# A graph network's sort with half of its keys in PSUM, its lists transposed ahead of the last raw products, and 14 raw rows instead of 11

## The reference

```python
h = relu(layernorm(x))
h = batchnorm(h, g0, b0)
for W1, b1, g, bt, W2, b2 in layers:        # two layers
    agg = segment_sum(h[src], dst, n)       # over the edges
    h = h + agg
    h = relu(batchnorm(h @ W1 + b1, g, bt))
    h = relu(h @ W2 + b2)
return x + h
```

## Time and profile before

| what | value |
|---|---|
| median of the runs | 2820.61 us |
| the profiled execution's own time | 2806.54 us |
| its span (first to last instruction) | 2804.7 us |
| busy: PE, DVE, ACT, POOL | 85%, 62%, 19%, 66% of the span |
| DMA | 735.46 MB, mean 262 GB/s |

### The profile page before, as it was taken

How to read it: one execution, slowest core, us unless ns; L and a number is a source line. 1 busy time by engine, 2 the same in 40 slices (tenths; PEclk the granted TensorE clock), 3 DMA queues, 4 the chain that set the end, 5 groups by cost and what they waited for, 6 DMA issues and landing times.

```text
span 2804.7 us, 30481 instructions
## 1 busy us (share of the span) xinstructions
PE 2380.3 (85%) x10221; PEld 1829.1 (65%) x10221; DVE 1734.9 (62%) x3349; ACT 528.8 (19%) x1542; POOL 1846.7 (66%) x1870
## 2 busy tenths in 40 slices
PE   1466657999999999999998666799999999989879
PEld 1133424788777777777776544588888888776767
DVE  6999995655555555555556577655555555544459
ACT  8963534300000000000007611100000000000038
POOL 2058886777777777777770277777777777777720
PEclk8685766999999999999998899999999999999999
DMA  9387994888888888888874999988888888888868
GB/s 307 144 263 203 300 311 123 254 267 254 254 254 254 254 254 253 254 254 254 253 242 161 338 354 353 301 282 288 284 284 287 284 283 287 259 254 254 253 204 271
DMA packets 309073, 735.46 MB, mean 262 GB/s; under 512 B 41126, under 2 KB 183346, under 8 KB 308910
## 3 DMA queue, kind: packets, MB, share of 16 engines
q0 software_dynamic: 148896, 552.17, 62.7%
q1 hardware_dynamic: 160014, 181.25, 20.0%
HBM read 580.67 MB, written 152.59 MB: 261 GB/s over the span
## 4 chain that ended last, share of the span: by engine, by line
PE 49%; DMA 21%; POOL 13%; SPq 7%; issue 5%; ACT 5%; DVE 1%; DVEq 0%; ACTq 0%; POOLq 0%
PE agg_ps L815 33%; DMA rows<-node_rows,src_all 19%; POOL rows L687 8%; SPq L610 7%; PE mm_ps L940 6%; PE mm_ps L857 5%; POOL rows L672 3%; PE mm_ps L861 2%; POOL raw_more L672 2%; ACT acc L985 2%; ACT lane_code L972 1%; PE agg_ps L769 1%; ACT lane_code L961 1%; DMA raw_more<-node_rows,src_all 1%; DMA node_rows<-acc 1%
## 5 line engine op out<-in xcount | busy, mean ns | idle before, releaser
L687 POOL DMA_INDIRECT rows<-node_rows,src_all x1672 | 1580.4, 945 | 647.6 <-issue 347.9
L815 PE MATMUL agg_ps<-rows,work 128*128 128x256 f32 (+1 forms) x7106 | 1662.4, 387 | 179.7 <-DMA rows<-node_rows,src_all 136.0
L815 PEld LDWEIGHTS agg_ps<-rows,work 128*128 128x128 f32 x7106 | 1311.0, 190 | 502.9 <-DMA rows<-node_rows,src_all 122.9
L1514 DVE SCALAR_TENSOR_TENSOR acc<-agg_ps,in_first,acc 128x256 f32 (+1 forms) x289 | 140.0, 485 | 955.9 <-PE agg_ps L815 880.7
L1016 ACT ACTIVATE bn_root<-bn_var 128x2 f32<-128x2 f32 x3 | 0.6, 204 | 1891.1 <-DVE bn_var L1146 1891.1
L672 POOL DMA_INDIRECT rows<-node_rows,src_all x96 | 137.2, 1429 | 166.2 <-DMA node_rows<-acc 137.2
L1466 DVE TENSOR_TENSOR work<-lane_code,lane_ps 128x1024 f32<-128x1024 f32 (+1 forms) x209 | 231.6, 1108 | 1.1 <-issue 1.1
L940 PE MATMUL mm_ps<-early,work 128*128 128x256 f32 x784 | 176.1, 389 | 20.0 <-ACT work L1095 11.4
L940 PEld LDWEIGHTS mm_ps<-early,work 128*128 128x128 f32 x784 | 141.0, 194 | 55.3 <-issue 23.4
L1475 DVE TENSOR_TENSOR work<-lane_code,lane_ps 128x640 f32<-128x640 f32 x209 | 169.8, 812 | 0.0
L1095 ACT ACTIVATE work<-acc,bn_shift,bn_scale 128x128 f32<-128x128 f32 x392 | 167.3, 485 | 3.3 <-DVE bn_shift L1157 2.8
(11 more groups left out here) (250 smaller groups left out, 1663.7 us busy)
## 6 DMA issues: line engine op xcount, KB each, us to landing
node_rows<-acc SPq DMA_DIRECT2D x113, 260.0 KB, 5.7
rows<-node_rows,src_all POOLq DMA_INDIRECT x1768, 4.3
node_rows<-acc SPq DMA_DIRECT2D x27, 910.0 KB, 4.3
node_rows<-acc SPq DMA_DIRECT2D x57, 390.0 KB, 5.9
node_rows<-acc SPq DMA_DIRECT2D x28, 650.0 KB, 7.7
node_rows<-acc SPq DMA_DIRECT2D x114, 130.0 KB, 4.6
acc<-in_x SPq DMA_DIRECT2D x13, 896.0 KB, 11.0
rows<-in_x SPq DMA_DIRECT2D x13, 896.0 KB, 7.4
```

Source lines behind the costliest of these rows:

```text
L687: pool.indirect_dma_start(tile_rows(k, 0, ROWS_OF[t] * DP), None, tables[layer][0:NPOS if t >= LAST_STRIDED else TABLE, :], bass.IndirectO ...
L815: mm = pe.matmul(bank[:, 0:width], hot[:, unit * P:(unit + 1) * P], tile_rows(k, row, width), start=(start and n == 0), stop=(stop and n = ...
L1514: dve.scalar_tensor_tensor(to, sums, lanes[:, g:g + 1], to, ALU.mult, ALU.add).then_inc(sums_added, 1)
```

## The change

- **Sort.** The first 45 steps of the first sort stay in SBUF (`in_sbuf`), now from `other` to `keys`. Its last 21 steps and the whole second sort (`split_steps`) keep half of the keys in SBUF and half in a PSUM tensor of four banks, `sort_ps`: a step reads the low partners from SBUF and the high ones from PSUM, and writes its results as minimum and maximum for each of two halves, four instructions of 512 elements. The last step of a sort writes all to `keys` in two instructions of 1024. Between the sorts, the differences of neighbours (`steps_ints`, before in `keys`) lie in `sort_ps`.
- **PSUM.** `sort_ps` takes the place of `tr_ps` and `mm_ps`; pairs get two banks (`PB` = 2) instead of four, and raw sums two instead of three.
- **Lists.** PE transposes the lists after raw group 54 of 56 (`LISTS_AT`), sources first; ACT copies the sources at once, and POOL's walk gathers wait for that copy (`src_ready`) and the transposes instead of `walk_ready`. A gather that would land on raw buffers waits for the last raw product (`FIRST_OVER_RAWS`). ACT's copies of lanes and DVE's of codes wait for the last raw product too.
- **Raw rows.** 14 instead of 11: 224 raw gathers, and a walk of 96 rows in layer 0. The strided copies are spread over 208 raw tiles instead of 144.
- **Places** of LayerNorm's steps in the first sort: variances at instruction 18 and 54 instead of 10 and 48, the rest at 30 and 62 instead of 22 and 56.

```diff
-PB = 4
+PB = 2
-LN_VAR_AT = (10, 48)
-LN_REST_AT = (22, 56)
-RAWS = 11
+LN_VAR_AT = (18, 54)
+LN_REST_AT = (30, 62)
+RAWS = 14
+LISTS_AT = RAW_GROUPS - 2
-FIRST_LANES_AT = 64
+FIRST_LANES_AT = 72
-COPIES_UNTIL = RAW_TILES - 2 * RAW
+COPIES_UNTIL = RAW_TILES - RAW
...
-            pool.wait_ge(walk_ready, 1)
+            pool.wait_ge(src_ready, 1)
+            pool.wait_ge(lists_transposed, 1)
...
+                if k == FIRST_OVER_RAWS:
+                    pool.wait_ge(raw_done, RAW_TILES)
...
             for n in range(RAW_GROUPS):
+                if n == LISTS_AT:
+                    transpose_lists()
                 sum_raw_group(n)
...
+            def halves(sbuf, i):
+                return (sbuf[:, i * SORT // 2:(i + 1) * SORT // 2], sort_ps[:, i * SORT // 2:(i + 1) * SORT // 2])
+            def split_steps(half, of, sbuf, to):
+                turn = 0
+                while half < SORT:
+                    by = half
+                    while by:
+                        if of is None:
+                            lows, highs = [t.rearrange("p (n k) -> p n k", k=by) for t in halves(sbuf, turn)]
+                            turn = 1 - turn
...
+                        after()
+                        if by == 1 and half == SORT // 2:
+                            outs = to.rearrange("p (n k) -> p n k", k=2)
+                            step(dve.tensor_tensor(outs[:, :, 0:1], lows, highs, ALU.min))
+                            step(dve.tensor_tensor(outs[:, :, 1:2], lows, highs, ALU.max))
+                        else:
+                            for i, out in enumerate(halves(sbuf, turn)):
+                                for m, op in enumerate((ALU.min, ALU.max)):
+                                    if by > 1:
+                                        place = out.rearrange("p (n m k) -> p n m k", m=2, k=by // 2)[:, :, m, :]
+                                    else:
+                                        place = out.rearrange("p (n r m) -> p n r m", m=2, r=half)[:, :, :, m]
+                                    low, high = pairs_of(by, i)
+                                    step(dve.tensor_tensor(place, low, high, op))
...
-            sort_rows(beside_first)
+            runs = in_sbuf(other, keys, SORT // 4, beside_first)
+            dve.wait_ge(raw_taken, 1)
+            split_steps(SORT // 4, keys, other, keys)
...
-            step(dve.tensor_tensor(key_ints[:, 1:SORT], other_ints[:, 1:SORT], other_ints[:, 0:SORT - 1], ALU.subtract))
+            step(dve.tensor_tensor(steps_ints[:, 1:SORT], other_ints[:, 1:SORT], other_ints[:, 0:SORT - 1], ALU.subtract))
...
-            step(dve.tensor_tensor(keys, second, keys, ALU.max))
-            sort_rows()
+            for i, out in enumerate(halves(other, 0)):
+                part = slice(i * SORT // 2, (i + 1) * SORT // 2)
+                step(dve.tensor_tensor(out, second[:, part], keys[:, part], ALU.max))
+            split_steps(1, None, other, keys)
```

More of the change, by code:

```diff
@@ L193 @@
 place_tiles()
+FIRST_OVER_RAWS = next(k for k, (_, _, t) in enumerate(TILES) if (TILE_AT[k] + ROWS_OF[t]) * DP > 4 * SORT)
 X_SLOTS = 4
@@ L759, in sum_raw_group @@
                 bank = early_ps[g % len(early_ps)]
-                if first == 0 and g == len(early_ps) - 1:
-                    pe.wait_ge(bn_centred, 1)
                 if first == 0 and g >= len(early_ps):
@@ L944, in _ @@
             pe.wait_ge(walk_ready, 1)
+            pe.wait_ge(raw_kept, RAWS)
             for layer in range(2):
@@ L1062, in _ @@
                     hot_of_raw(n + RAW_HOTS)
-                if n % ROW_GROUPS == ROW_GROUPS - 1:
+                if n == LISTS_AT - 1:
+                    bn_root_of(0)
+                    act.wait_ge(src_transposed, 1)
+                    for bank, first, end in SRC_LIST:
+                        ins = act.copy(by_tile(src_all, T)[:, first:end, :], bank_tiles(bank)[:, 0:end - first, :])
+                    ins.then_inc(src_ready, 1)
+                if n % ROW_GROUPS == ROW_GROUPS - 1 and n < RAW_GROUPS - 1:
                     keep_raw(n // ROW_GROUPS)
-            bn_root_of(0)
             act.wait_ge(lists_transposed, 1)
-            for to, banks in ((src_all, SRC_LIST), (lane_all, LANE_LIST)):
-                for bank, place, first, end in banks:
-                    ins = act.copy(by_tile(to, T)[:, first:end, :], bank_tiles(bank)[:, place:place + end - first, :])
+            act.wait_ge(raw_done, RAW_TILES)
+            for bank, first, end in LANE_LIST:
+                ins = act.copy(by_tile(lane_all, T)[:, first:end, :], bank_tiles(bank)[:, 0:end - first, :])
             ins.then_inc(lists_ready, 1)
+            keep_raw(RAWS - 1)
             def add_self(layer):
@@ L1263, in _, with in_sbuf @@
             dve.wait_ge(setup_done, done)
-            step(dve.scalar_tensor_tensor(keys[:, 0:LR], self_edges, REMOVED, keys[:, 0:LR], ALU.mult, ALU.add))
-            def sort_rows(beside=None):
-                of, to = keys, other
+            step(dve.scalar_tensor_tensor(other[:, 0:LR], self_edges, REMOVED, keys[:, 0:LR], ALU.mult, ALU.add))
+            def in_sbuf(of, to, runs, beside):
                 half, n = 1, 0
-                while half < SORT:
+                while half < runs:
                     by = half
@@ L1285, in sort_rows, with pairs_of @@
                     half *= 2
-                assert of is keys
-            sort_rows(beside_first)
+                return of
+            def halves(sbuf, i):
[9 more added lines that the diff above has]
+                        else:
+                            both = of.rearrange("p (n k) -> p n k", k=2 * by)
+                            lows, highs, of = both[:, :, 0:by], both[:, :, by:2 * by], None
+                        def pairs_of(cut, i):
+                            if by > 1:
+                                first, end = i * by // 2, (i + 1) * by // 2
+                                if by < half:
+                                    return lows[:, :, first:end], highs[:, :, first:end]
+                                last = by - 1 - first
+                                return lows[:, :, first:end], highs[:, :, last:last - by // 2 if last >= by // 2 else None:-1]
+                            return [t.rearrange("p (n c r) k -> p n c (r k)", c=2, r=half)[:, :, i, :] for t in (lows, highs)]
+                        after()
[6 more added lines that the diff above has]
+                                for m, op in enumerate((ALU.min, ALU.max)):
+                                    if by > 1:
+                                        place = out.rearrange("p (n m k) -> p n m k", m=2, k=by // 2)[:, :, m, :]
+                                    else:
+                                        place = out.rearrange("p (n r m) -> p n r m", m=2, r=half)[:, :, :, m]
+                                    low, high = pairs_of(by, i)
+                                    step(dve.tensor_tensor(place, low, high, op))
+                        by //= 2
+                    half *= 2
@@ L1290, in _ @@
+            runs = in_sbuf(other, keys, SORT // 4, beside_first)
+            dve.wait_ge(raw_taken, 1)
+            assert runs is keys
+            split_steps(SORT // 4, keys, other, keys)
+            steps_ints = sort_ps_ints
             a, b, second = temps[0], temps[1], temps[2]
@@ L1325, in _ @@
             after()
-            step(dve.scalar_tensor_tensor(parts, parts, 1.0, key_ints, ALU.add, ALU.mult))
+            step(dve.scalar_tensor_tensor(parts, parts, 1.0, steps_ints, ALU.add, ALU.mult))
             after()
@@ L1438, in _ @@
             dve.wait_ge(lists_transposed, 1)
+            dve.wait_ge(raw_done, RAW_TILES)
             for bank, first, end in CODE_LIST:
-                if end == len(CODED):
-                    dve.wait_ge(lists_ready, 1)
-                ins = dve.tensor_copy(by_tile(code_all, len(CODED))[:, first:end, :], bank_tiles(bank)[:, 0:end - first, :])
-            ins.then_inc(walk_ready, 1)
+                step(dve.tensor_copy(by_tile(code_all, len(CODED))[:, first:end, :], bank_tiles(bank)[:, 0:end - first, :]))
+            after()
+            dve.wait_ge(lists_ready, 1)
+            dve.tensor_copy(lane_ps[:, 0:2 * P], iota_row[:, :]).then_inc(walk_ready, 1)
             def shift_of_h():
```

98 lines of the change are left out of this document (52 added, 46 removed).

## The result

The changed kernel takes 2784.12 us (2783.2 to 2784.4, four runs) against 2820.36 (2819.3 to 2820.8) of the kernel before in the same batch of runs: a ratio of 0.987, 95% interval 0.986 to 0.989. The forecast was 2786. Its profiled execution took 2784.43 us with a span of 2782.6.

The account below looks back on a forecast made before the run. POOL's gathers were taken to bound the walk, set by its first gather and row count. An earlier first gather (-7.9), three rows fewer (-30.0) and 3 us given back made -34.9, forecast 2786 us, range 2776 to 2814.

Parts of the forecast that it names:

- Sort step: Both sorts on DVE: a step of four 512 instructions takes 2.55 us instead of 2.40, 0.15 us more.
- rival of the late sort: Second sort: PSUM access at every second word costs 25 to 33 us, total 2808 to 2816; chance 0.20 for 2800 to 2817.
- DVE's waits in the first sort: First sort: with LayerNorm's steps moved later, DVE no longer waits for ACT, -6.5 us.
- Between the sorts: DVE between the sorts: two one-input instructions lose their double rate because the differences lie in PSUM, +2.1 us.
- Raw gathers: POOL beside the sorts: 224 instead of 176, 1.25 us each without two SBUF inputs on DVE; POOL free at 467.
- 3 us for DMA: Second sort: DMA is asked for 3% more than it moved, so 3 us added, POOL free at 470.
- Lists ahead of the last products: PE after raw group 54 of 56: lists ready for POOL at 466, first walk gather at 470, 7.9 us earlier.
- Three rows: Layer 0's walk: three rows fewer, 24 gathers of 1.25 us, -30.0 us.
- Given back: Start of the walk: PE starts about 12 us behind the first gather, POOL waits 0 to 7 us, taken as 3.
- Sum: Whole kernel: -7.9 - 30.0 + 3 = -34.9 us, 2771.6 from the profiled execution, 2786 from the median.
- gathers not relieved: Raw gathers: any busy DVE or its writes hold POOL, pace stays as before, +20 us, 2841; chance 0.04.
- PSUM at half pace: Sort steps: DVE reading and writing PSUM takes two cycles a word, +91 us, 2874; chance 0.06.

Follow-up runs that it names:

- x6: Changed kernel with LayerNorm's steps at their old places in the first sort (10, 48 and 22, 56): 2782.10 us.
- x2: Changed kernel with 11 raw rows again, sorts half in PSUM and early lists kept: 2806.05 us, ratio 0.994 to the kernel before.
- x3: Changed kernel with the second sort wholly in SBUF again, two instructions of 1024 a step: 2821.22 us, ratio 1.000 to the kernel before.
- x5: Changed kernel with the lists transposed behind the last raw product, as before the change: 2786.86 us, ratio 0.991 to the kernel before.
- x4: Kernel before with 14 raw rows and nothing else changed: 2850.31 us, ratio 1.011.
- x8: Changed kernel with layer 1's two natural tiles of 90 rows instead of 80 gathered ahead of the strided ones: 2774.15 us.
- x9: Changed kernel run again unchanged, as the measure for later runs on the same chip: 2778.45 us, ratio 0.987 to the kernel before.
- x10: Changed kernel with layer 1's natural tiles of 90 rows instead of 80 first, repeated beside the unchanged changed kernel: 2774.67 us.
- x12: Changed kernel with natural tiles of 90 rows first and four more instructions between the sorts reading PSUM: 2770.16 us, ratio 0.984 to the kernel before.
- x7: Changed kernel with 13 raw rows instead of 14: 2780.87 us.
- x11: Changed kernel with natural tiles of 90 rows first in layer 1 and 13 raw rows instead of 14: 2774.69 us.

## Why the prediction was right

- *Sort step*, 2.55 us: 2.53. All patterns alike, so the rival of the late sort fell. What the Trainium skill says of gaps in matmuls (PSUM — Partial Sum Buffer, Specifications) is not seen on DVE here, nor are the extra cycles of a PSUM source in its table (VectorE: DVE Perf Modes, the TRN2 errata): 686 ns with an input in PSUM against 688 without.
- *DVE's waits in the first sort*, -6.5: none is left, and the sort ends at 201 (forecast 202). But here the reasoning had a loose end. I counted the term into the lists (460.9; they end at 458.96), and then let POOL, not the lists, set the first walk gather. x6 shows what the term is worth there: 1.7 us.
- *Between the sorts*, +2.1: the two instructions take 2.29 and 2.28 us, +2.1.
- *Raw gathers*: forecast 32 at the end of the first sort, 203 at the end of the second and POOL free at 467, 470 with 3 us for DMA. Measured 33, 202 and 469.07. The 3 us were mis-sized: DMA was 101% busy and cost nothing that shows, 136 gathers in 168 us; x2 has the same pace at 106%. The reading behind the 1.25, that two SBUF inputs hold a gather, is borne out by x3, where the holds come back with them. POOL was 2 us later than 467: at 461 there were 218 gathers out, not 219, and the last six took 7.5 us, where the sum has five in 6.
- *Lists ahead of the last products*: forecast 466 for POOL; ACT's copy ends at 464.42, and PE's wait held no gather. x5 shows that this part was needed: +9.9 us at the first gather without it.
- *Three rows*, -30.0: 24 gathers fewer at 1.25. That the last of the three brings only 0 to 2.4 us was not in my sum: the rows and the first gather hang together, since each row is 10 us less of walk and 20 us more of raw gathers, which cost nothing only as long as POOL waits for the lists anyway.
- *Given back*, 3: PE's first product of the walk came 10.2 us behind the first gather (forecast 12), and POOL waited 2.5 us for PE between 610 and 633 and lost 0.8 on longer gathers.
- *Sum*, -34.9: the last gather of layer 0 comes 35.8 us earlier, the medians differ by 36.2. Carrying the difference over to the median was right by luck as much as by reason: that the profile's own 14 us were mostly one wait in layer 1, I had not looked for.

The other rivals: *gathers not relieved* is refuted by the pace (1.24 us); x3 and x4, where the second sort doesn't relieve them, lie on both sides of its 2841 (2821 with the early lists, 2850 without). *PSUM at half pace* is refuted by the 690 ns of an instruction that reads and writes PSUM.

## What to carry to other kernels

Where POOL issues gathers all the time, ask of every DVE instruction beside them where its operands lie: one of two in PSUM lets the gathers pass, and a slower DVE instruction can be the better one. Such a relief is worth only what the freed engine can be given to do; without the three rows, relief and early lists brought 15 us (which the lists alone may have brought), with them 36, and the rows alone cost 29.5. And before a difference is carried over from one profiled execution, look for waits on DMA that one execution has and another has not.

## What the runs showed of the hardware that I had not expected

**What frees the gathers is a PSUM input, not a PSUM output.** DVE between the sorts of the changed kernel, and POOL beside it:

```profile
203.64 2.30 DVE L1364 TENSOR_TENSOR sort_ps<-work 128x2047 int32<-128x2047 int32 x1
205.98 2.29 DVE L1366 TENSOR_SCALAR rows<-sort_ps 128x2048 f32<-128x2048 int32 x1
208.19 2.28 DVE L1367 TENSOR_SCALAR rows<-sort_ps 128x2048 int32<-128x2048 int32 x1
...
217.48 4.42 DVE L1375 TENSOR_TENSOR_SCAN rows<-rows 128x2048 f32<-128x2048 f32 x1
```

```profile
203.97 2.79 POOL L679 DMA_INDIRECT rows<-node_rows,raw_list  x1 [0.30 <-issue]
207.06 0.94 POOL L679 DMA_INDIRECT rows<-node_rows,raw_list  x1 [0.30 <-issue]
208.31 0.94 POOL L679 DMA_INDIRECT rows<-node_rows,raw_list  x1 [0.30 <-issue]
...
218.31 4.35 POOL L679 DMA_INDIRECT raw_more<-node_rows,raw_list  x1 [0.30 <-issue]
```

The instruction at 203.64 writes PSUM from two SBUF inputs and the gather beside it takes 2.79 us; those that read PSUM hold none; the scan of two SBUF inputs holds one for 4.35. No semaphore stands between these gathers and DVE. What I wrote ahead of the prediction, that the engines meet only at semaphores, is not so here.

Why does only every third gather take 1.97 us beside the sort in SBUF? The sort instructions that stand beside the four raw gathers of x3 above:

```profile
300.96 1.22 DVE L1298 TENSOR_TENSOR work<-work 128x1024 f32<-128x1024 f32 x1
303.36 1.22 DVE L1298 TENSOR_TENSOR work<-work 128x1024 f32<-128x1024 f32 x1
304.61 1.23 DVE L1296 TENSOR_TENSOR work<-work 128x1024 f32<-128x1024 f32 x1
305.75 1.22 DVE L1298 TENSOR_TENSOR work<-work 128x1024 f32<-128x1024 f32 x1
```

The two gathers that are held (301.03, 305.82) start 0.07 us behind the start of an instruction and end 0.82 us behind its end; the two that pass (303.30, 304.56) start 0.05 or 0.06 us ahead of one. In the second sort of the kernel before it is so for all 33 that are held (0.05 to 0.07 us behind) and all 66 that pass (0.03 to 0.06 ahead). Two sort steps take 4.79 us, and so do three gathers of which one is held, so the pattern repeats. In the changed kernel's second sort the gathers start at any distance behind an instruction's start, and none is held.

The Trainium skill (SBUF — State Buffer, the section on SBUF's two separate sides) says that a DVE instruction in a two-port mode, or one with two SBUF inputs beside a GpSimd operation that reads SBUF, and the GpSimd operation lock a shared pair of ports: whichever starts first has it for its whole instruction, and the other is blocked. For the gathers beside the sort the runs agree, with the distances above. That a gather which starts first blocks DVE they don't show there: a sort step takes 2.39 to 2.40 us beside the gathers and also before the first of them, from 130 to 160.

**DVE stops for 2 to 3 us where no semaphore holds it.** DVE's statistics ahead of layer 1's normalisation, changed kernel:

```profile
1453.88 0.25 DVE L1147 BATCH_NORM_STATS2 bn_stats<-acc 128x6 f32<-128x84 f32 x1 [3.02 <-issue]
1456.41 0.25 DVE L1147 BATCH_NORM_STATS2 bn_stats<-acc 128x6 f32<-128x84 f32 x1 [2.28 <-issue]
```

All that its DMA moved in the 6.5 us around (queue, kind: packets, MB, share of 16 engines):

```profile
q14 instruction: 2, 0.02, 0.9%
```

In the kernel before there is one such stop:

```profile
1490.39 0.39 DVE L1125 BATCH_NORM_STATS2 bn_stats<-acc 128x6 f32<-128x84 f32 x2 [3.02 <-issue]
```

DVE waits for nothing that the profile shows, and the two packets are of the instruction queue. Right ahead of the first stop the record of DVE's sequencer has a branch: the test at L1687 (L1619 in the kernel before) by which DVE skips its general path, at 1451.02 in the changed kernel and at 1487.53 in the kernel before, 2.9 us before the next instruction in both (2.9 to 3.1 in all profiles). A second stop of 2.1 to 2.2 us is in the profiles of x5, x6, x8, x9, x10 and x12 too, one of 1.56 us in x3, and none in the kernels with 11 or 13 rows, nor in x4. It comes one or two instructions later, without a branch. It is 2.1 of the 3.5 us that x7 gained on x9 between the layers, and 2.2 of the 4.6 that x11 gained on x10; the rest is not explained. That DVE waits for its code to be loaded, after the branch and once more, is read from the DMA row and not shown; no run was made to test it.
